# Weaving a narrow attention head between the chunks of a wide one

## What is computed

```python
scores = einsum('bqhd,bkhd->bhqk', q, k) / sqrt(head_dim)
scores = scores + slopes[None, :, None, None] * -abs(pos[None, :] - pos[:, None])
probs = softmax(scores, axis=-1)
out = einsum('bhqk,bkhd->bqhd', probs, v).reshape(B, L, D)
return out @ Wout + bout
```

## Time and profile before

| | |
|---|---|
| median of 3 runs | 1075.12 us (1073.6 to 1075.43) |
| the profiled execution, own time | 1074.98 us |
| its span in the profile | 1073.2 us |
| mean granted TensorE clock | 0.977 |
| TensorE busy | 1027.0 us, 96% |
| ScalarE busy | 813.8 us, 76% |
| VectorE busy | 437.6 us, 41% |
| GpSimd busy | 306.6 us, 29% |
| instructions | 39594 |

### The profile page before, as it was taken

The page is one execution under the profiler, slowest core; times in us unless marked ns, Lnnn a source line. Parts: engine busy times, 40 slices in busy tenths (PEclk is TensorE's granted clock), DMA queues, the critical chain, the costliest instruction groups (busy, mean ns, idle before and its releaser), DMA issues. The chain is left out here.

```text
span 1073.2 us, 39594 instructions
## 1 busy us (share of the span) xinstructions
PE 1027.0 (96%) x17563; PEld 729.3 (68%) x17563; DVE 437.6 (41%) x1030; ACT 813.8 (76%) x807; POOL 306.6 (29%) x454
## 2 busy tenths in 40 slices
PE   9999899999999999999999999999996389999997
PEld 6555676776676786877766766878685346666665
DVE  5777334452342332235434623324257511111165
ACT  3564799999999999999999999999966164111252
POOL 3333122122121121112221521211330345554433
PEclk9999999999999999999999999999999579999998
DMA  5765312112222111112242121220209245544473
GB/s 193 221 189 170 110 54 78 57 54 78 61 60 58 51 50 44 51 45 75 87 118 61 57 70 51 64 58 16 86 14 313 40 124 169 127 113 111 115 279 133
DMA packets 76558, 104.81 MB, mean 98 GB/s; under 512 B 13774, under 2 KB 62556, under 8 KB 76380
## 3 DMA queue, kind: packets, MB, share of 16 engines
q1 hardware_dynamic: 65852, 87.94, 26.4%
q0 software_dynamic: 6080, 9.06, 4.1%
q10 hardware_dynamic: 4448, 5.19, 1.6%
HBM read 66.49 MB, written 31.48 MB: 91 GB/s over the span
## 5 line engine op out<-in xcount | busy, mean ns | idle before, releaser
L1021 ACT ACTIVATE prob<-ps 128x1536 f32<-128x1536 f32 (+5 forms) x489 | 662.2, 1515 | 16.7 <-PE ps L977 15.1
L977 PE MATMUL ps<-q_stack,k_stack 99*32 99x128 bf16 (+17 forms) x8949 | 460.1, 294 | 4.6 <-ACT prob L1021 3.0
L1001 PE MATMUL ps<-prob,v_head 128*32 128x128 f32 (+7 forms) x7288 | 457.6, 338 | 1.7 <-issue 1.7
L977 PEld LDWEIGHTS ps<-q_stack,k_stack 123*32 123x32 bf16 (+4 forms) x8949 | 269.7, 96 | 130.0 <-ACT prob L1021 69.3
L1001 PEld LDWEIGHTS ps<-prob,v_head 128*32 128x32 f32 x7288 | 283.7, 109 | 53.9 <-issue 8.4
L1031 POOL TENSOR_TENSOR prob<-prob,near_bias 128x128 f32<-128x128 f32 x256 | 127.0, 500 | 520.3 <-ACT prob L1021 520.3
L1031 DVE TENSOR_TENSOR prob<-prob,near_bias 128x128 f32<-128x128 f32 x256 | 81.9, 327 | 421.0 <-ACT prob L1021 421.0
L1049 DVE RECIPROCAL o_rec<-o_den 128x128 f32<-128x128 f32 x128 | 113.8, 925 | 0.7
L1726 PE MATMUL ps<-xeT,w 128*128 128x512 f32 x224 | 100.0, 604 | 0.8 <-ACT xeT L1757 0.7
L1803 ACT ACTIVATE hT<-ps 128x512 f32<-128x512 f32 x28 | 16.7, 596 | 110.4 <-PE ps L1726 99.4
L1740 PE MATMUL ps<-w,hT 128*128 128x256 f32 x448 | 99.6, 384 | 0.0
(11 more groups left out here) (173 smaller groups left out, 613.3 us busy)
## 6 DMA issues: line engine op xcount, KB each, us to landing
qk_parts<-split SPq DMA_DIRECT2D x32, 384.0 KB, 3.2
w<-L_ffn_experts_inter_dram SPq DMA_DIRECT2D x7, 1024.0 KB
w<-n_L_ffn_experts_out_dram SPq DMA_DIRECT2D x7, 1024.0 KB
q_stack<-qk_parts SPq DMA_DIRECT2D x31, 192.0 KB
k_stack<-qk_parts SPq DMA_DIRECT2D x31, 192.0 KB
z_rows<-v SPq DMA_DIRECT2D x8, 516.0 KB, 10.0
heads<-o_out SPq DMA_DIRECT2D x128, 32.0 KB, 2.5
v<-in_L_attn_x_dram SPq DMA_DIRECT2D x8, 512.0 KB, 6.0
```

The source lines that it names most:

```text
L977: mm = pe.matmul(ps[k:k + keys, SLOT_BANKS * (c % 2) + bank, col:col + z - a], k_st[n % STACKS][0:rows, kb * P + k:kb * P + k + keys], q_s ...
L1001: mm = pe.matmul(ps[32 * g:32 * g + 32, 6 + n % 2, column:column + width * times], vh[n % 2][:, kb, :], moving, start=(n, g) not in begun, ...
L1021: act.activation(prob[:, c % RING, 0:at + z - a], ps[:, bank:bank + SLOT_BANKS, :].rearrange("p c n -> p (c n)")[:, 0:at + z - a], ACT.Exp ...
```

## The change

`packed` is gone. Each pair of items has chunks of its own: `woven` cuts the wide item into chunks of 1536 columns and lets its last, partial one be the start of the narrow item's first chunk; `evenly` cuts the narrow item into chunks as few as possible and as equal as possible. The chunks of the narrow item are put between those of the wide one, from the wide chunk with index NARROW_FROM = 6 on or a little later, so that the narrow item is through three chunks before the wide one. Both items of a pair thus accumulate at once, in banks 6 and 7. `place_of` gives each item its bank and its buffer of v, so that the wide item of a pair takes the place of the narrow one before, and `place_user_before` says whom it has to wait for. As items end in another order than they begin, `ENDING` and `RANK` give this order to the division and the stores. A chunk with two items is scored in strips if one of its heads is 5 or more. Values of every chunk are done in a burst of their own. The last four bias additions go to the chunks 13, 10, 7 and 4 before the end.

```diff
--- before.py
+++ after.py
@@ -47,6 +47,7 @@
 PV_LAG = 5
 VALUE_LAG = 4
 IN_STRIPS = 5
+NARROW_FROM = 6
 STACKS = 3
 
 ST = CAP // P
@@ -111,17 +112,27 @@
     return max((at + z - a for _, _, a, z, at in chunk), default=0)
 
 
-def packed(items):
-
-    chunks = [[]]
-    for n, (b, h) in enumerate(items):
-        at = filled(chunks[-1])
-        mine = next(new for new in (fill(n, h, at, more) for more in range(0, P, 16))
-                    if n + 1 == len(items) or filled(new[-1]) % P == 0)
-        chunks = chunks[:-1] + [chunks[-1] + mine[0]] + mine[1:]
-        if filled(chunks[-1]) == WIDTH:
-            chunks.append([])
-    return [chunk for chunk in chunks if chunk]
+def evenly(n, h, at):
+
+    columns = at + sum(z - a for _, a, z in spans(h, 0))
+    count = -(-columns // WIDTH)
+    widths = range(-(-columns // count // 16) * 16, WIDTH, 16)
+    return fill(n, h, at, 0, next((w for w in widths if w >= at and len(fill(n, h, at, 0, w)) == count), WIDTH))
+
+
+def woven(wide, narrow):
+
+    first = fill(*wide, 0, 0)
+    at = sum(z - a for *_, a, z, _ in first[-1])
+    second = evenly(*narrow, at)
+    wide_chunks, narrow_chunks = first[:-1], [first[-1] + second[0]] + second[1:]
+    chunks, done = [], 0
+    for r, chunk in enumerate(wide_chunks):
+        chunks.append(chunk)
+        due = max(0, r + 2 - NARROW_FROM) * len(narrow_chunks) // (len(wide_chunks) - NARROW_FROM - 2)
+        chunks += narrow_chunks[done:due]
+        done = max(done, due)
+    return chunks
 
 
 def own_column(piece):
@@ -167,7 +178,7 @@
 
 
 ITEMS = [(b, h) for b in range(B) for heavy in range(H // 2, H) for h in (heavy, heavy - H // 2)]
-CHAIN = packed(ITEMS)
+CHAIN = [chunk for n in range(0, len(ITEMS), 2) for chunk in woven((n, ITEMS[n][1]), (n + 1, ITEMS[n + 1][1]))]
 CHUNK_COUNT = len(CHAIN)
 
 
@@ -177,6 +188,21 @@
 
 USES = [[c for c in range(CHUNK_COUNT) if n in items_of(c)] for n in range(len(ITEMS))]
 FIRST, LAST = [uses[0] for uses in USES], [uses[-1] for uses in USES]
+ENDING = sorted(range(len(ITEMS)), key=lambda n: LAST[n])
+RANK = [ENDING.index(n) for n in range(len(ITEMS))]
+
+
+def place_of(n):
+
+    return (n // 2 + n % 2) % 2
+
+
+def place_user_before(n):
+
+    earlier = [m for m in range(len(ITEMS)) if place_of(m) == place_of(n) and LAST[m] < FIRST[n]]
+    return max(earlier, key=lambda m: LAST[m]) if earlier else None
+
+
 
 
 def own_blocks(c, odd):
@@ -184,18 +210,18 @@
     return [(ITEMS[piece[0]][1], own_column(piece)) for piece in CHAIN[c] if own_column(piece) is not None and piece[1] % 2 == odd]
 
 
-BIAS_AT = [FIRST[-8] + 3 * c for c in range(QG)] + [FIRST[-1] + 3 * c for c in range(QG)]
+BIAS_AT = [FIRST[-8] + 3 * c for c in range(QG)] + [CHUNK_COUNT - 13 + 3 * c for c in range(QG)]
 
 
 def scores_in_strips(c):
-    return ITEMS[items_of(c)[0]][1] >= IN_STRIPS
+    return max(ITEMS[n][1] for n in items_of(c)) >= IN_STRIPS
 
 
 def value_bursts():
 
     bursts, done = [], 0
     for c in range(CHUNK_COUNT):
-        due = c - VALUE_LAG + 1 if scores_in_strips(c) or c % 2 == 1 else done
+        due = c - VALUE_LAG + 1
         bursts.append(range(done, max(done, due)))
         done = max(done, due)
     return bursts, range(done, CHUNK_COUNT)
@@ -209,7 +235,7 @@
     plan, line = [[] for _ in range(CHUNK_COUNT + len(ITEMS) * (2 + QG))], []
     for slot in range(len(plan)):
         if slot - VALUE_LAG - 2 in LAST:
-            n = LAST.index(slot - VALUE_LAG - 2)
+            n = RANK[LAST.index(slot - VALUE_LAG - 2)]
             plan[slot].append((n, TAKE))
             line += [(n, SPREAD)] + [(n, INVERT + q) for q in range(QG)] + [(n, SCALE)]
         elif line:
@@ -918,7 +944,7 @@
 
     def banded_sync(sp):
         def store_turned_heads(n):
-            b, h = ITEMS[n]
+            b, h = ITEMS[ENDING[n]]
             sp.wait_ge(o_ready, n + 1)
             at = h * HD % P
             turned = heads[at:at + HD, h * HD // P, b * L:(b + 1) * L].rearrange("d (j g i) -> d g j i", g=GROUPS, i=P)
@@ -990,16 +1016,16 @@
             for n in items_of(c):
                 if c == FIRST[n]:
                     pe.wait_ge(vh_done, n + 1)
-                    if n >= 2:
-                        pe.wait_ge(o_read, n - 1)
+                    if place_user_before(n) is not None:
+                        pe.wait_ge(o_read, RANK[place_user_before(n)] + 1)
             for g, n, kb, at, column, width, times in value_turns(CHAIN[c]):
                 slab = prob[:, c % RING, :]
                 if times > 1:
                     moving = bass.AP(slab.tensor, slab.offset + at, [slab.ap[0], [GROUPS * P, times], [1, P]])
                 else:
                     moving = slab[:, at:at + width]
-                mm = pe.matmul(ps[32 * g:32 * g + 32, 6 + n % 2, column:column + width * times],
-                               vh[n % 2][:, kb, :], moving, start=(n, g) not in begun, stop=False,
+                mm = pe.matmul(ps[32 * g:32 * g + 32, 6 + place_of(n), column:column + width * times],
+                               vh[place_of(n)][:, kb, :], moving, start=(n, g) not in begun, stop=False,
                                skip_group_check=True)
                 begun.add((n, g))
             mm.then_inc(pv_done, 1)
@@ -1032,10 +1058,10 @@
 
     def banded_vector(dve):
         def take(n):
-            dve.wait_ge(pv_done, LAST[n] + 1)
+            dve.wait_ge(pv_done, LAST[ENDING[n]] + 1)
             if n >= 2:
                 dve.wait_ge(o_ready, n - 1)
-            dve.tensor_copy(o_sb[n % 2][:, :], ps[:, 6 + n % 2, :]).then_inc(o_read, 1)
+            dve.tensor_copy(o_sb[n % 2][:, :], ps[:, 6 + place_of(ENDING[n]), :]).then_inc(o_read, 1)
 
         def spread(n):
             dve.wait_ge(o_read, n + 1)
@@ -1078,9 +1104,9 @@
                 if c != FIRST[n]:
                     continue
                 b, h = ITEMS[n]
-                if n >= 2:
-                    pool.wait_ge(pv_done, LAST[n - 2] + 1)
-                pool.tensor_copy(vh[n % 2][:, :, 0:HD], t["v"][:, b * KB:(b + 1) * KB, h * HD:(h + 1) * HD])\
+                if place_user_before(n) is not None:
+                    pool.wait_ge(pv_done, LAST[place_user_before(n)] + 1)
+                pool.tensor_copy(vh[place_of(n)][:, :, 0:HD], t["v"][:, b * KB:(b + 1) * KB, h * HD:(h + 1) * HD])\
                     .then_inc(vh_done, 1)
             near_blocks(pool, c, 1, diag_odd)
             if c in BIAS_AT:
```

## The result

The changed kernel takes 1184.09 us (median of 4 runs, 1183.68 to 1185.68) against 1074.36 us (1073.47 to 1075.43) before: 1.103 times as long, with a 95% interval of 1.101 to 1.104. The forecast was 1162 us, in a range of 1131 to 1182. Slower it was, and by the mechanism that was written down; but the time lies 2 us beyond the range, and the loss is 110 us where 87 were forecast. The profiled execution has a span of 1183.9 us, 110.7 more than before.

The account below looks back on a forecast made before the run. ScalarE's exponentials, at 1.34 us a chunk, were taken to bound the stage. Stack wait +69.0, clock +19.6, weaving -4.1 and end +2.5 made +87.0 on 1074.98 us: 1162 us, range 1131 to 1182.

Parts of the forecast that it names:

- wait for the stack: Narrow heads' first chunks: TensorE and ScalarE wait 3.6 to 6.3 us for the load in 14 pairs, +69.0 us.
- the clock: After 14 waits TensorE's granted clock falls, 1.4 us each: +19.6 us, bounds 0 and twice that.
- the longer end: After the last exponential: two divisions on VectorE instead of one before the router, +2.5 us, bounds 0 and 5.5.
- the load: An item's eleven DMAs into its stack take about 14.8 us from first issue, slowed by two engines at the end.
- weaving: Narrow chunks between wide ones: of 17.4 us lost at narrow heads 13.3 remain, -4.1 us, bounds -8 and +5.
- high end: Top of the range, 1182 us: long loads (+7) and the clock at two thirds more than priced (+13).
- values in single bursts belong to the same term: Values of each chunk in one burst: no separate price, since the 1.57 us slot has one burst.
- count as covered by the wide chunks between: Narrow heads' loss beyond 0.23 us per lone full-width chunk, including strip-scored heads 5 to 7, taken as covered: -4.1 us.
- Costed at nothing: VectorE's copy, GpSimd's copy of v, stores, loads of x and later bias additions: 0 us in the sum.
- That the clock stays up: Rival: in the stack waits the clock does not fall, or its fall ends inside them; 1142 us, chance 0.25.
- That nothing waits: Rival: the load is in before the narrow head's first chunk; 1073.5 to 1078 us, chance 0.06.
- That each wait is half as long: Rival: ScalarE has chunks in hand, so waits halve; +34 us and some clock, 1110 to 1125 us, chance 0.07.

Follow-up runs that it names:

- b_single: The kernel before, with values in single bursts everywhere and nothing else changed: 1079.35 us, 1.0032 of before.
- w4: The changed kernel with a fourth pair of stacks (STACKS 4 instead of 3): 1084.16 us, 1.0084 of before.
- busy: The changed kernel with 14, 20 or 28 matmuls of no use ahead of the wait for the narrow head's stack: 1160.09 us.
- b4: The kernel before with four stacks instead of three and nothing else changed: 1076.17 us, 0.9998 of before.

## Why the prediction was wrong, and where it was right

The mechanism was right: the wait for the stack, the fall of the clock behind it, and the longer end are all there. Sizes failed, and one sign: the load (14.8 us, measured 15.5), the clock (1.4 us a pair, measured 2.0 or more), and weaving (-4.1 us, measured as a loss together with the single bursts that it took in). The steps of the change follow each other in kernels that differ by one part each. In the profiled executions:

| step | forecast | whole stage | behind the first eleven chunks | from |
|---|---|---|---|---|
| single bursts | in weaving | +3.3 | +2.9 | before to b_single |
| weaving, own chunks | -4.1 with bursts | -1.4 | +0.5 | b_single to w4 |
| wait for the stack | +69.0 | +76.7 | +74.8 | w4 to busy |
| clock | +19.6 | +27.6 | +29.0 | busy to after |
| first eleven chunks | 0 | in the above | -1.0 | before to after |
| end of the stage to the router | +2.5 | +3.8 | +3.8 | before to after |
| all else | 0 | +0.7 | +0.7 | rest of the span |
| sum | +87.0 | +110.7 | +110.7 | |

The first eleven exponentials lie ahead of every wait for a stack, yet differ between executions, because the clock sometimes falls there and sometimes does not. The exponentials alone, in w4 and in b_single, where the twelfth begins within the window (length, ScalarE busy, clock, DMA share, GB/s):

```profile
113.88:128.58 14.70, 14.69 (x11) 1.00 0.33 103
```

```profile
115.27:132.06 16.79, 15.38 (x12) 0.80 0.35 97
```

The eleven take 14.69 and 16.80 us. That is 2.1 us, of which 0.2 are columns (w4 has 256 fewer in these chunks), and it is not weaving's. The third column of numbers leaves it out.

**The range.** Its high end gave long loads 7 us and the clock 13, together 20. Wait and clock came 15.7 above their terms (76.7 and 27.6), within that. What carried the time past the end was weaving, for which the high end had nothing: bursts and weaving together are +1.9 in the whole stage, 6.0 above -4.1, and +3.4 behind the first eleven chunks. The end gave another 1.3, the rest 0.7.

**The stacks: right, the load too short.** SP's wait for LAST[n-3], the k of each pair, the 14 breaks and pair 8 without one came as worked out. Off was the size of one term: the load. I read its end from the window in which the DMA share went out, 14.8 us; the changed kernel shows 15.5, in which the last packet ends at 400.33 and TensorE's first weights are loaded at 400.91. That half a microsecond between the last packet and TensorE's start is not in windows of DMA share. A load longer by 0.7 us makes 14 x 0.7 = 9.8 us by the prediction's formula, and the term came out 7.7 larger than forecast. Of the 2.1 between (4.0 by the third column, 74.8), 1.4 are in pair 12: the break behind VectorE's copy lies inside its load, so that less of the load was left to wait for.

**The clock: right in kind, a third too small.** The 1.4 us came from the start of the stage, where the low clock lasted 3.4 us and part of it fell into work that ScalarE could cover. After the long waits TensorE ran at 1.2 GHz for up to five microseconds with no scores in hand, and it cost 27.6 / 14 = 2.0 us a pair, or 2.1 for each of the 13 falls. The bound of twice the price held it. By the Trainium skill (TensorE: Matmul & The Clock Gate, HAM oscillation) such waits make each burst start cold; 13 of the 14 waits agree, the one in which TensorE stood idle for 3.62 us does not.

**Weaving: wrong in sign.** The step that failed is "values in single bursts belong to the same term". They are a term of their own, +3.3 (+2.9), for which the one slot of 1.57 us could not stand: it has a wide chunk's values behind a narrow score. And what the prediction did "count as covered by the wide chunks between" was to give 4.1 and gave nothing: -1.4 by the whole stage, +0.5 without the start. Against the kernel before, head 3 and head 4 lost a microsecond or so each (the full-width chunks come every second or third slot there, and it may be that two wide ones do not give back 0.23 us; no run shows it), heads 5 and 6 gained about half a microsecond and a quarter.

**The end: right in kind.** The first copy was to begin 1 us ahead of the last exponential's end; it began 0.2 ahead (897.18), since the values of chunk 490 were not through. From the router's start to the end of the span it is 274.5 us before, 275.0 after, 277.5 to 278.0 in the five experiments that weave the last pair, and 275.5 to 276.3 in the four that do not: up to 3.5 us more, which the prediction did not have and no run explains.

**Costed at nothing.** In w4 VectorE's copy ahead of the values was hidden in every pair but one; there it stood behind a block that lasted as long as GpSimd's bias addition, and cost 1.4 us. The loads of x: the break of 2.1 us that stood at 771.90 is in none of the woven kernels, where the prediction had it as unchanged. In b_single it is still there, 2.0 us, and in b4, 1.65 us. What sets it was not tried. Between b_single and w4 these two breaks come and go, +1.4 and -2.0, so that weaving's own part is about 1 us of loss.

**The rivals.** That the clock stays up, at 0.25, was wrong. That nothing waits, at 0.06, is the case only with a fourth stack, as in w4, and even then it is 1084 us, not 1073.5 to 1078. That each wait is half as long, at 0.07, was wrong: the breaks have their full length.

## What to carry to other kernels

When work is moved earlier, ask first for its inputs: a ring of buffers was deep enough for one order of the work and is not for another, and the number that decides is the distance, in slots, between the last use of a buffer and the first use of its next content, against the time from issue to first use. A wait of a few microseconds of TensorE costs its own length and, where the clock falls, a good third more; a change that puts one in each round of a loop is dear by both. And a slack that an order leaves is worth only what the bottleneck engine lacks: here ScalarE was busy for 98% of the stage, so that weaving could bring at most the other 14 us, and brought none of them.

## What the runs showed that was not expected

An item's load with twelve DMAs of one part of 16 rows is in after 11.0 us, where six DMAs of 3, 2 and 1 parts took 15.5, for the same bytes and with six more to issue. Matmuls of no use that keep TensorE busy in a wait took 24 us off the whole kernel. Single bursts of values cost 3.3 us where full-width chunks come in rows and save 4.7 us where they stand alone: the same line has two signs. And a multiply on VectorE that began during GpSimd's bias addition never ended before it: 1.5 to 1.8 us instead of 0.29 in w4, which is nothing as a rule and 1.4 us where a copy that TensorE waits for stands behind it.
